# A four-layer network on one core: the first layer's experts run on the tokens that chose them, in 23 sorted tiles

## The chip, the cores and the metric

One core of one Trainium2 chip. The metric is the time of one execution in microseconds (us), the slowest core's, here the only one's. All data is 32-bit floating point unless a row says otherwise. Engines: PE (TensorE, matrix products), DVE (VectorE), ACT (ScalarE), POOL (GpSimd), SP (SyncE, which only issues transfers). PEld is PE's loading of the stationary operand.

## The reference, cut to what matters

Four layers, each `x = x + s * silu(g)` on 1024 tokens of 256 numbers, where `s` comes from a mixer and `g` from a feed-forward part, both of the normed `x`. The change touches only the first layer:

```python
# mixer: xh = xn @ W_in + b_in; gates by two block-diagonal products and sigmoid;
# complex decay a = exp(...), xc = sqrt(1 - a*a) * (xr + i*xi) * gate_x; h = linear scan of (a, xc) over 256 steps
# s = concat(h.real, h.imag) @ W_out + b_out
def _L0_ffn_ref(...):                       # 8 experts, each token takes 2
    shared = silu(x @ shared_gate_w) * (x @ shared_up_w) @ shared_down_w
    logits = x @ router_w
    top_val, top_idx = jax.lax.top_k(logits, K)                       # K = 2
    probs = jnp.zeros_like(logits).at[jnp.arange(T)[:, None], top_idx].set(jax.nn.sigmoid(top_val))
    xin = probs.T[:, :, None] * x[None]
    gu = jnp.einsum('etd,edf->etf', xin, gate_up_w)                   # 256 -> 2 * 128
    gate, up = jnp.split(gu, 2, axis=-1)
    h = jax.nn.silu(gate) * up
    expert_out = jnp.einsum('eti,eid->etd', h, down_w)                # 128 -> 256
    return shared + expert_out.sum(axis=0)
```

A token's weight is zero for the six experts that it did not choose, so their part of the sum is zero.

## The kernel before

Tokens are held as 8 tiles of 128 (`x_tok`, `xn_tok`), and turned, with features on the partitions, as `xnT`. PSUM is one tensor `banks` of 8 banks of 512 columns. The program is a row of stages (blocks); at the end of each all engines meet. The first block loads `x` and the first layer's weights: SP and ACT issue the transfers (ACT those of the list `late0`, L2796), and ACT then fetches its table of functions and warms it (L2798). `norm_stage` norms and turns `x`. Then `recurrent_layer_stage` does the whole first layer.

In that stage each engine has its own program, in the order in which it is written; semaphores join them. PE: `xh` (L444) with the router's logits (L450) between, the gates (L461), the turned choice weights (L468), the shared expert, and then 16 jobs, one for each of 8 experts and each half (512) of the tokens: `raise_` (L413, four products of 512 columns: gate and up) and `lower` (L421, four of 256 columns, summed in banks 0 to 3). DVE ranks the logits by comparing all pairs (`rank_mask`), then does the recurrence (about 35 operations of 128x1024, two scans and two reciprocals among them). Between its operations it does, for each job, `weigh` (L585, L587: gate and up times the token's weight) and `hidden` (L595). ACT does the sigmoids, sines and roots (`root`, L511) and each job's Silu (L507). The weights of the choices reach all partitions through DRAM (`probs_dram`). At the end PE multiplies `hT` by `W_out` (L489, `mix`), DVE and POOL add the bias (`add_bias`), DVE adds the gated result to `x_tok` (`add_gated`), and PE runs seven products on the identity that nothing reads (`keep_busy`, L494) before the stage's end.

The third layer's experts (L1370, L1843 and around) already gather tokens by an indirect transfer of POOL from `xn_dram`, with positions found by a running count (`top_mask`) and one-hot products.

## Time and profile before

| | us |
|---|---|
| median of 3 runs | 987.98 (985.75 to 992.25) |
| profiled execution, its time | 983.79 |
| its span, first to last instruction | 982.0 |
| PE busy | 922.5 (94%) |
| DVE busy | 685.5 (70%) |
| ACT busy | 478.2 (49%) |
| POOL busy | 289.7 (29%) |

The mean granted TensorE clock of the profiled execution is 0.995 of full speed. The first layer's stage runs from 15.6 to 142.2 us of the span. A row of the timeline gives start, duration, engine, line, operation, result<-operands with their shapes, a count of merged instructions, and in brackets how long the engine had sat idle before and what released it. `PEq`, `SPq` and so on are an engine's sequencer. One 32-bit product of 512 columns is two records of the trace.

### The profile page before, as it was taken

To read this page: it belongs to the slowest core of one execution; us is meant where nothing else is said; L and a number is where in the kernel's file an instruction comes from. 1 tells how busy PE (TensorE), PEld (TensorE's weight loads), DVE (VectorE), ACT (ScalarE), POOL (GpSimd) and SP (SyncE) were. 2 spreads that over 40 slices of the span, in tenths; PEclk is the share of its full clock that TensorE was granted. 3 is DMA by queue.
4 is the path that set the end of the run, shared out by engine and by line. 5 is a ranking of instruction groups with operands and counts; after the bars stand their busy time and mean duration, and the time that the engine had idled before them with its cause. 6 is when DMAs were issued, how large, how long until landed. Compare 5 with 4: busy or idle time off the path is not lost. (4 is left out here: it accounts for less than half of the span.)

```text
span 982.0 us, 13585 instructions
## 1 busy us (share of the span) xinstructions
PE 922.5 (94%) x4660; PEld 556.4 (57%) x4660; DVE 685.5 (70%) x1095; ACT 478.2 (49%) x1008; POOL 289.7 (29%) x254
## 2 busy tenths in 40 slices
PE   6999999999999999989999999989899899999997
PEld 3455564365566565655565555566466556555554
DVE  2889877368999999885635565576786735666552
ACT  3642224798888788444135555566665630111112
POOL 0000020007888788723013232103554420000000
PEclk9999999999999999999999999999999999999999
DMA  4123215041000000008454444201000002111101
GB/s 137 45 72 90 64 43 155 1 104 39 22 23 32 12 26 8 1 17 258 122 156 109 92 111 95 39 33 39 7 1 2 1 2 64 33 33 32 32 0 43
DMA packets 58303, 53.89 MB, mean 55 GB/s; under 512 B 14216, under 2 KB 53224, under 8 KB 58240
## 3 DMA queue, kind: packets, MB, share of 16 engines
q1 hardware_dynamic: 52704, 47.05, 16.2%
q0 software_dynamic: 3072, 4.20, 2.7%
q10 hardware_dynamic: 2464, 1.84, 0.6%
q8 instruction: 36, 0.59, 0.3%
q14 instruction: 27, 0.22, 0.1%
HBM read 44.45 MB, written 5.47 MB: 51 GB/s over the span
## 5 line engine op out<-in xcount | busy, mean ns | idle before, releaser
L1127 POOL TENSOR_TENSOR seen<-state,c_row 128x512 f32<-128x512 f32 x128 | 160.9, 1278 | 100.6 <-DVE state L1147 72.9
L1147 DVE TENSOR_TENSOR_SCAN state<-decay,banks 128x512 f32<-128x512 f32 x128 | 154.5, 1215 | 14.6 <-issue 7.1
L2646 PE MATMUL banks<-xnT,weight 128*128 128x512 f32 x256 | 115.2, 592 | 0.0
L1085 ACT ACTIVATE weighed_x<-dx_tok,b_tok 128x512 f32<-128x512 f32 x124 | 87.6, 709 | 26.4 <-PE banks L1263 25.1
L1095 ACT ACTIVATE decay<-delta_pairs,A 128x510 f32<-128x510 f32 x128 | 90.4, 707 | 6.2 <-DVE state L1147 6.2
L2299 POOL TENSOR_TENSOR prob<-prob,inverse 128x512 f32<-128x512 f32 x64 | 65.3, 1041 | 95.4 <-DVE inverse L2417 95.4
L1263 PEld LDWEIGHTS banks<-ident,weighed_x 128*128 128x128 f32 x512 | 58.3, 140 | 60.2 <-ACT weighed_x L1085 36.0
L2652 ACT ACTIVATE w_WqT<-banks 128x512 f32<-128x512 f32 x32 | 19.1, 597 | 149.2 <-PE banks L2646 149.2
L1263 PE MATMUL banks<-ident,weighed_x 128*128 128x128 f32 x512 | 80.1, 279 | 2.4 <-DVE state L1147 2.3
L2646 PEld LDWEIGHTS banks<-xnT,weight 128*128 128x128 f32 x256 | 48.6, 190 | 48.3 <-issue 46.7
L1277 PE MATMUL banks<-seen,fold 128*64 128x512 f32 x256 | 69.0, 618 | 0.0
L2658 DVE TENSOR_TENSOR inter<-w_WqT,banks 128x512 f32<-128x512 f32 x32 | 22.0, 688 | 66.7 <-ACT w_WqT L2652 66.1
L2480 ACT ACTIVATE prob<-banks,shift 128x256 f32<-128x256 f32 x128 | 59.2, 472 | 19.1 <-DVE probT L2424 9.0
L2017 DVE COPY probT<-banks 128x512 f32<-128x512 f32 x48 | 33.1, 690 | 45.2 <-PE banks L1891 40.6
L2704 PE MATMUL banks<-weight,inter 128*128 128x256 f32 x256 | 60.4, 379 | 1.1 <-PEq L2282 1.1
L2704 PEld LDWEIGHTS banks<-weight,inter 128*128 128x128 f32 x256 | 48.5, 190 | 20.9 <-issue 15.8
L413 PE MATMUL banks<-xnT,gate_up_w 128*128 128x512 f32 x128 | 57.6, 593 | 0.0
L2412 DVE TENSOR_REDUCE shift<-banks 128x2 f32<-128x512 f32 x64 | 40.9, 680 | 19.8 <-PE banks L2340 19.8
L2424 DVE STREAM_TRANSPOSE probT<-prob 128x512 f32<-128x512 f32 x64 | 44.1, 701 | 11.5 <-POOL prob L2299 11.5
L1843 POOL DMA_INDIRECT y_dram<-slot_result,slot_target x16 | 25.4, 1585 | 77.7 <-ACT slot_result L2092 77.7
L2073 ACT ACTIVATE prob<-banks,score_shift 128x128 f32<-128x128 f32 (+1 forms) x128 | 44.5, 423 | 1.4 <-DVE score_shift L2013 1.4
L2340 PE MATMUL banks<-latT,q_now 64*128 64x256 f32 x256 | 37.2, 409 | 7.7 <-ACT prob L2480 7.7
(395 smaller groups left out, 1687.9 us busy)
## 6 DMA issues: line engine op xcount, KB each, us to landing
prob_row<-probs_dram SPq DMA_DIRECT2D x8, 512.0 KB, 3.8
c_row<-c_dram SPq DMA_DIRECT2D x32, 128.0 KB, 2.9
slot_wide_w<-in_L_ffn_w_gate SPq DMA_DIRECT2D x16, 176.0 KB, 2.5
slot_wide_w<-in_L_ffn_w_up SPq DMA_DIRECT2D x16, 176.0 KB, 2.6
slot_down_w<-in_L_ffn_w_down SPq DMA_DIRECT2D x16, 176.0 KB
gate_up_w<-in_L_ffn_gate_up_w SPq DMA_DIRECT2D x8, 256.0 KB, 3.0
delta_pairs<-conv_in SPq DMA_DIRECT2D x8, 256.0 KB, 3.5
w_WqT<-in_L_attn_W_q SPq DMA_DIRECT2D x1, 2048.0 KB, 12.9
```

The source lines that it names most:

```text
L413: last = nc.tensor.matmul(banks[:, 4 + 2 * half + j, :], wide(j, k), xnT[:, k, cols[half]], start=(k == 0), stop=(k == KD - 1))
L1085: nc.scalar.activation(weighed[:, v % 2, tile, :, j, :], dx_tok[:, 4 * p + tile, :].rearrange("p (g e) -> p g e", g=groups), ACT.Identity, ...
L1095: nc.scalar.activation(decay[:, u % ring, :, 1:], delta[:, g, cols[p]].rearrange("p (b t) -> p b t", b=BATCH // 2)[:, :, 1:], ACT.Exp, sca ...
L1127: nc.gpsimd.tensor_tensor(seen[:, u % ring, :], state[:, u % ring, :], c_row[:, v % 4, :], ALU.mult).then_inc(seen_ready, 1)
L1147: nc.vector.tensor_tensor_scan(state[:, u % ring, :], decay[:, u % ring, :, :].rearrange("p b t -> p (b t)"), banks[:, 4 + u % 2, :], 0.0, ...
L1263: last = nc.tensor.transpose(banks[:, 4 + u % 2, tile * P:(tile + 1) * P], weighed[:, v % 2, tile, g, :, :].rearrange("p j e -> p (j e)"), ...
L1277: nc.tensor.matmul(banks[half, g // 2, :], fold[:, :], seen[:, u % ring, :], start=False, stop=(pair == STATES // 2 - 1), skip_group_check ...
L2073: last = nc.scalar.activation(dst[:, h, :], bank[:, h, :], ACT.Exp, bias=shift[:, u % 8, h:h + 1])
L2299: nc.gpsimd.tensor_tensor(two, two, inverse[:, u % 2, h, :].unsqueeze(2).broadcast_to([P, 2, SEQ]), ALU.mult).then_inc(prob_ready, 1)
L2480: last = nc.scalar.activation(prob[:, u % 2, h, qt * SEQ:(qt + 1) * SEQ], score_bank(u, h)[:, qt * SEQ:(qt + 1) * SEQ], ACT.Exp, bias=shif ...
L2646: last = self.nc.tensor.matmul(self.banks[:, pair + j, :], self.weights.weight[:, s, j, k, tile * P:(tile + 1) * P], self.xnT[:, k, self.c ...
L2704: last = nc.tensor.matmul(banks[:, t // 2, (t % 2) * D:(t % 2 + 1) * D], jobs.inter[:, tile, t * P:(t + 1) * P], weight[:, s, 2, tile, :], ...
```

## The change

The choices (2 of each of 1024 tokens, 2048 in all) are sorted by expert. Each expert's choices are padded up to tiles of 128 rows; (2048 + 8 * 127) / 128 gives at most 23 tiles. The number of tiles is fixed, whatever the data; a register holds each tile's expert, and the products take their weights at that register's address. All eight experts' weights now lie in SBUF. Tiles go in 12 groups of two (the last of one).

- SP stores the normed tokens to DRAM, loads all expert weights in 8 transfers, and stores each group's result rows to DRAM.
- DVE's routing is new: `top_mask`, a running place of every choice, then one-hot tensors; PE turns them by 16 products into a table (which token and which weight each slot of each tile has). PE reads 23 expert numbers into registers, then `keep_busy` with 4 products.
- POOL gathers 23 tiles of token rows. For a group: `turn_x` (PE), `keep_xT` (ACT), `raise_` (PE), `gate` (ACT, Silu with the slot's weight as scale), `middle` (DVE), `turn_mid` (PE), `keep_midT` (ACT), `lower` (PE), `keep_result` (ACT), store (SP). PE and ACT take the steps of several groups in turn; the 12 `middle` stand at fixed places in DVE's recurrence.
- When all results are stored, POOL gathers each token's two rows back: 16 transfers. PE adds them to the shared expert's part by products with the identity (`add_rows`). The bias is added by PE as well, into the banks of `mix`, so `add_bias` goes.
- ACT's list `late0` gets three more loads (`before`, `slots`, `choice_token`).

```diff
--- before.py
+++ after.py
...
-    jobs = 2 * (experts + 1)
+    choices = top * NT
+    tiles = (top * N + experts * (P - 1)) // P
+    groups = -(-tiles // 2)
+    size = [min(2, tiles - 2 * g) for g in range(groups)]
+    ring = 4
...
+                sp.dma_start(xn_dram.rearrange("(n p) d -> p n d", p=P), xn_tok[:, :, :]).then_inc(xn_stored, DMA)
+                for e in range(0, experts, 2):
+                    two = slice(e, e + 2)
+                    sp.dma_start(gate_up_w[:, two, :].rearrange("p e (k n) -> p (e k) n", k=KD),
+                                 gate_up[two, :, :].rearrange("e (k p) n -> p (e k) n", p=P)).then_inc(expert_weights_loaded, DMA)
+                    sp.dma_start(down_w[:, two, :], down[two, :, :].rearrange("e p n -> p e n")
+                                 ).then_inc(expert_weights_loaded, DMA)
+                for g in range(groups):
+                    sp.wait_ge(result_ready, g + 1)
+                    sp.dma_start(rows_dram[2 * g * P:(2 * g + size[g]) * P, :].rearrange("(a p) d -> p a d", p=P),
+                                 result[:, g % ring, 0:size[g], :]).then_inc(stored[g % ring], DMA)
...
+                def turn_x(g):
+                    pe.wait_ge(gathered[g % ring], DMA * tiles_to(g))
+                    if g >= 2:
+                        pe.wait_ge(xT_ready, g - 1)
+                    for k in range(KD):
+                        for j in range(size[g]):
+                            c = (2 * k + j) * P
+                            ins = nc.tensor.transpose(banks[:, g % 2, c:c + P], slot_x[:, g % ring, j, k * P:(k + 1) * P],
+                                                      ident[:, :])
+                    ins.then_inc(x_turned, 1)
...
+                def raise_(g):
+                    pe.wait_ge(xT_ready, g + 1)
+                    if g >= 2:
+                        pe.wait_ge(mid_ready, g - 1)
...
+                            ins = nc.tensor.matmul(
+                                banks[:, 2 + g % 2, j * 2 * width:(j + 1) * 2 * width], slot_xT[:, g % 2, k, j, :],
+                                gate_up_w[:, bass.ds(expert[2 * g + j], 1), k * 2 * width:(k + 1) * 2 * width].rearrange(
+                                    "p e n -> p (e n)"), start=(k == 0), stop=(k == KD - 1))
+                    ins.then_inc(raised, 1)
...
+                def add_rows(b):
+                    pe.wait_ge(rows_gathered[b], 2 * top * DMA)
+                    for t in (2 * b, 2 * b + 1):
+                        for r in range(top):
+                            ins = nc.tensor.matmul(banks[:, b, (t % 2) * D:(t % 2 + 1) * D], ident[:, :], rows[:, t, r, :],
+                                                   start=False, stop=(r == top - 1), skip_group_check=True)
+                    ins.then_inc(summed, 1)
...
+                pe.wait_ge(entries_ready, 2)
+                for n in range(choices):
+                    if n % (choices // 2) == 0:
+                        pe.wait_ge(one_hot_ready, n // (choices // 2) + 1)
+                    ins = nc.tensor.matmul(banks[:, 1, 0:2 * tiles], one_hot[:, n, :],
+                                           entry[:, n, :, :].rearrange("p i a -> p (i a)"), start=(n == 0), stop=(n == choices - 1))
+                ins.then_inc(table_done, 1)
+                pe.wait_ge(expert_index_ready, 1)
+                expert = [pe.value_load(expert_index[0:1, a:a + 1], min_val=0, max_val=experts - 1) for a in range(tiles)]
+                keep_busy(nc, banks[:, 3, :], ident, 4)
+                pe.wait_ge(expert_weights_loaded, DMA * experts)
+                turn_x(0)
+                pe.wait_ge(slot_prob_ready, 1)
+                for s in range(groups + 2):
+                    if s + 1 < groups:
+                        turn_x(s + 1)
+                    if s < groups:
+                        raise_(s)
+                    if s == 1:
+                        pe.wait_ge(shared_ready, 2)
+                    if 1 <= s <= groups:
+                        turn_mid(s - 1)
+                    if s >= 2:
+                        lower(s - 2)
+
+                pe.wait_ge(xT_ready, groups)
...
+                for b in range(2):
+                    add_rows(b)
                 pe.wait_ge(h_ready, 2)
-                for t in range(NT):
-                    for k in range(KD):
-                        last = nc.tensor.matmul(
-                            banks[:, 4 + t // 2, (t % 2) * D:(t % 2 + 1) * D], hT[:, k, t * P:(t + 1) * P],
-                            w["W_out"][:, k, :], start=(k == 0), stop=(k == KD - 1))
-                    last.then_inc(mixed, 1)
+                mix(0)
+                add_rows(2)
+                mix(1)
+                add_rows(3)
+                mix(2)
+                mix(3)
                 pe.wait_ge(gate_ready, 1)
                 keep_busy(nc, banks[:, 0, :], ident, 7)
...
+                for s in range(groups + 2):
+                    if s + 1 < groups:
+                        keep_xT(s + 1)
+                    if s < groups:
+                        gate(s)
+                    if 1 <= s <= groups:
+                        keep_midT(s - 1)
+                    if s >= 2:
+                        keep_result(s - 2)
+                    if s == 2:
+                        for q in range(4):
+                            act.wait_ge(angles_ready, q + 1)
+                            nc.scalar.activation(wave[:, q, :], wave[:, q, :], ACT.Sin, scale=two_pi).then_inc(waves_ready, 1)
+                    if s in (5, 6):
+                        root(s - 5)
...
+                pool.wait_ge(xn_stored, DMA)
+                pool.wait_ge(slot_token_ready, 1)
+                for a in range(tiles):
+                    g = a // 2
+                    if g >= ring:
+                        pool.wait_ge(x_turned, g - ring + 1)
+                    pool.indirect_dma_start(out=slot_x[:, g % ring, a % 2, :], out_offset=None, in_=xn_dram[:, :],
+                                            in_offset=bass.IndirectOffsetOnAxis(ap=slot_token[:, a:a + 1], axis=0)
+                                            ).then_inc(gathered[g % ring], DMA)
+                pool.wait_ge(row_index_ready, 1)
+                for r in range(ring):
+                    pool.wait_ge(stored[r], DMA * len(range(r, groups, ring)))
+                for t in range(NT):
+                    for r in range(top):
+                        pool.indirect_dma_start(out=rows[:, t, r, :], out_offset=None, in_=rows_dram[:, :],
+                                                in_offset=bass.IndirectOffsetOnAxis(ap=row_index[:, t, r:r + 1], axis=0)
+                                                ).then_inc(rows_gathered[t // 2], DMA)
 
             @block.vector
             def _(dve):
...
+                def middle(g):
+
+                    dve.wait_ge(silu_ready, g + 1)
+                    if g >= 2:
+                        dve.wait_ge(mid_turned, g - 1)
+                    for j in range(size[g]):
+                        ins = vector.scalar_tensor_tensor(
+                            mid[:, g % 2, j, :], banks[:, 2 + g % 2, j * 2 * width + width:(j + 1) * 2 * width],
+                            slot_prob[:, 2 * g + j:2 * g + j + 1], silu[:, g % 2, j, :], ALU.mult, ALU.mult)
+                    ins.then_inc(mid_ready, 1)
...
+                dve.wait_ge(table_done, 1)
+                vector.tensor_copy(slot_token[:, :], banks[:, 1, 0:tiles]).then_inc(slot_token_ready, 1)
+                vector.tensor_copy(slot_prob[:, :], banks[:, 1, tiles:2 * tiles]).then_inc(slot_prob_ready, 1)
+                dve.wait_ge(slot_prob_ready, 1)
...
+                shared(0)
+                shared(1)
+                angle(0)
+                angle(1)
+                middle(0)
...
+                steps.do(vector.tensor_tensor(ta[:, :], zr[:, :], zr[:, :], ALU.mult))
+                vector.tensor_tensor(ta[:, :], ta[:, :], tb[:, :], ALU.add).then_inc(square_ready, 1)
+                middle(4)
+                middle(5)
                 dve.wait_ge(modulus_ready, 1)
-                steps.do(nc.vector.tensor_tensor(tb[:, :], tc[:, :], zr[:, :], ALU.add))
-
-                nc.vector.tensor_scalar(ta[:, :], tb[:, :], 0.5, 1e-30, ALU.mult, ALU.max).then_inc(square_ready, 1)
-                hidden(2)
-                weigh(3)
+                steps.do(vector.tensor_tensor(tb[:, :], tc[:, :], zr[:, :], ALU.add))
+                vector.tensor_scalar(ta[:, :], tb[:, :], 0.5, 1e-30, ALU.mult, ALU.max).then_inc(square_ready, 1)
+                middle(6)
                 dve.wait_ge(modulus_ready, 2)
-                steps.do(nc.vector.reciprocal(tb[:, cols[0]], tc[:, cols[0]]))
-                hidden(3)
...
                 both(tb[:, :], zi[:, :], ALU.mult, sin)
-                hidden(7)
-                weigh(8)
+                middle(11)
                 both(tc[:, :], zi[:, :], ALU.mult, cos)
...
+    for name in ("before", "slots", "choice_token"):
+        add(name, list(A[name].shape), A[name], late)
```

The order of instructions at three places. First the start of ACT's queue, in the block before `norm_stage`: the last loads of `late0`, then the table and its warm-up (ACT's last work in the block). Before:

```order
L2796 DMA w_shared_up_w<-in_L_ffn_shared_up_w 128x2x128
L2796 DMA w_shared_down_w<-in_L_ffn_shared_down_w 128x256
L2798 ACT_TABLE_LOAD
L2798 ACTIVATE root_table<-root_table 128x1
L2777 UNCONDITIONAL_BRANCH
```

and of the change:

```order
L2954 DMA w_shared_down_w<-in_L_ffn_shared_down_w 128x256
L2954 DMA w_before<-in_before 128x128
L2954 DMA w_slots<-in_slots 128x128
L2954 DMA w_choice_token<-in_choice_token 128x16
L2956 ACT_TABLE_LOAD
L2956 ACTIVATE root_table<-root_table 128x1
```

Three issues now stand ahead of the table. Second, PE from the shared expert to its first routed products. Before (`L413` is `raise_`, `L421` is `lower`):

```order
L468 MATMUL banks<-ident,probs 8x128 x8
L413 MATMUL banks<-xnT,w_shared_gate_w 128x512 x2
L413 MATMUL banks<-xnT,w_shared_up_w 128x512 x2
L413 MATMUL banks<-xnT,gate_up_w 128x512 x4
L421 MATMUL banks<-w_shared_down_w,expert_hT 128x256 x4
```

and of the change (`L540` is the table, `L544` the read of a register, 23 times this load and pair in a row; `L437` is `turn_x`, `L447` `raise_`):

```order
L474 MATMUL banks<-xnT,w_shared_up_w 128x512 x2
L540 MATMUL banks<-entry,wave 128x46 x16
L544 TENSOR_LOAD tile_expert_index
L544 ISA x2
...
L242 MATMUL banks<-ident 128x512 x4
L437 MATMUL banks<-ident,slot_x 128x128 x8
L447 ISA
L447 MATMUL banks<-gate_up_w,slot_xT 128x256
```

Routed products followed the shared ones directly; now the table, the registers, `keep_busy` and two groups' gathered rows stand between. Third, DVE from the recurrence's first operation on. Before:

```order
L618 TENSOR_SCALAR turns<-gate_a,coef 128x1024
L620 SCALAR_TENSOR_TENSOR phi<-inside,turns 128x1024
L621 TENSOR_SCALAR ta<-turns 128x1024
L629 TENSOR_SCALAR tb<-ta 128x1024
L630 TENSOR_TENSOR angle<-ta,tb 128x1024
```

and of the change (`L798` waits for PE's table, `L720` is `middle`):

```order
L796 TENSOR_SCALAR turns<-gate_a,coef 128x1024
L798 CAST slot_token<-banks 128x23
L799 COPY slot_prob<-banks 128x23
L711 TENSOR_TENSOR shared_hT<-shared_silu,banks 128x512 x2
L804 TENSOR_SCALAR ta<-turns 128x1024
...
L720 SCALAR_TENSOR_TENSOR expert_mid<-banks,slot_prob,expert_silu 128x128 x2
L820 SCALAR_TENSOR_TENSOR phi<-inside,turns 128x1024
```

The wait for the table and the first `middle` now stand ahead of the scan `phi`.

## Rows read from the trace of the kernel before

**Rows 1.** Busy time by stretch (count of instructions), clock, DMA share, GB/s
```profile
70.00:120.00 50.00, 50.00 (x156) 28.69 (x155) 49.45 (x56) 13.35 (x16) 0.00 (x0) 1.00 0.25 76
```

**Rows 2.** Timeline, PE's job late in the stage, and the router's products
```profile
61.68 3.60 PE L413 MATMUL banks<-xnT,gate_up_w 128*128 128x512 f32 x8
65.11 1.89 PE L421 MATMUL banks<-down_w,expert_hT 128*128 128x256 f32 x8
66.84 3.60 PE L413 MATMUL banks<-xnT,gate_up_w 128*128 128x512 f32 x8
...
20.09 0.95 PE L450 MATMUL banks<-w_router_w,xnT 128*128 128x8 f32 x8
```

**Rows 3.** Timeline of DVE: a job's operations and the recurrence's
```profile
37.78 0.69 DVE L629 TENSOR_SCALAR tb<-ta 128x1024 f32<-128x1024 f32 x1
...
66.08 3.35 DVE L663 RECIPROCAL tb<-tc 128x512 f32<-128x512 f32 x1 [2.47 <-ACT tc L511]
...
85.31 0.68 DVE L595 TENSOR_TENSOR expert_hT<-expert_silu,expert_up 128x512 f32<-128x512 f32 x1
...
87.11 1.21 DVE L569 TENSOR_TENSOR zi<-radius,turns 128x1024 f32<-128x1024 f32 x1
...
103.00 2.28 DVE L701 TENSOR_TENSOR_SCAN zi<-radius,tc 128x1024 f32<-128x1024 f32 x1
```

**Rows 4.** Timeline of the stage's end and the next one's start
```profile
128.02 7.07 PE L489 MATMUL banks<-w_W_out,hT 128*128 128x256 f32 x32
...
137.51 3.60 PE L242 MATMUL banks<-ident 128*128 128x512 f32 x8
...
142.26 1.96 PE L242 MATMUL banks<-ident 128*128 128x512 f32 x4 [1.16 <-PEq L2814]
```

**Rows 5.** Timeline of the program's start, ACT's last loads and the first meeting
```profile
5.49 0.63 ACTq L2796 DMA_DIRECT2D w_shared_down_w<-in_L_ffn_shared_down_w  x1
...
6.15 1.28 ACT L2798 ACT_TABLE_LOAD   x1 [6.15 <-issue]
...
7.99 0.64 DVE L127 BATCH_NORM_AGGREGATE mean_var<-x_stats 128x2 f32<-128x6 f32 x8 [1.05 <-PEq L2777]
```

**Rows 6.** Timeline of the third layer's routing: a small operation of DVE
```profile
453.86 0.29 DVE L220 TENSOR_TENSOR above<-score,best 128x128 f32<-128x128 f32 x1
```

**Rows 7.** Timeline of the third layer's first gathers; last, all 16 as a group
```profile
499.45 1.17 POOL L1370 DMA_INDIRECT slot_x<-xn_dram,slot_token  x1 [38.60 <-DVE slot_token L1700]
...
500.93 0.97 POOL L1370 DMA_INDIRECT slot_x<-xn_dram,slot_token  x1 [0.30 <-issue]
...
502.46 0.44 PE L1944 MATMUL banks<-ident,slot_x 128*128 128x128 f32 x2 [1.06 <-DMA slot_x<-xn_dram,slot_token]
...
L1370 POOL DMA_INDIRECT slot_x<-xn_dram,slot_token x16 | 15.9, 997 | 53.6 <-DVE slot_token L1700 38.6 <-PE banks L1944 10.1 <-PE banks L1961 2.5
```

**Rows 8.** Transfers by line: count, KB each, median us from issue to landing
```profile
w_norm_w<-in_L_attn_norm_w SPq DMA_DIRECT2D x1, 1.0 KB, 1.7
...
out_dram<-x_tok SPq DMA_DIRECT2D x4, 256.0 KB, 2.1
```

**Rows 9.** Timeline of SP: an issue at a register's address
```profile
62.63 0.38 SPq L376 DMA_DIRECT2D gate_up_w<-in_L_ffn_gate_up_w  x1
```

**Rows 10.** ACT's groups: busy us, mean ns of one, idle before and its releaser
```profile
L2073 ACT ACTIVATE prob<-banks,score_shift 128x128 f32<-128x128 f32 x64 | 18.2, 374 | 1.4 <-DVE score_shift L2013 1.4
...
L2097 ACT ACTIVATE s_tok<-banks 128x512 f32<-128x512 f32 x3 | 1.8, 597 | 4.4 <-PE banks L1936 4.4
```

**Rows 11.** Timeline of ACT: a root of the recurrence
```profile
65.00 1.06 ACT L511 ACTIVATE tc<-ta 128x1024 f32<-128x1024 f32 x1
```

**Rows 12.** Timeline, DVE beside POOL and alone
```profile
133.72 1.27 POOL L272 TENSOR_TENSOR x_tok<-x_tok,s_tok 128x512 f32<-128x512 f32 x1
...
133.91 1.62 DVE L258 TENSOR_TENSOR x_tok<-x_tok,gated 128x512 f32<-128x512 f32 x1
...
136.95 0.69 DVE L258 TENSOR_TENSOR x_tok<-x_tok,gated 128x512 f32<-128x512 f32 x1
```

More of the change, by code:

```diff
@@ L481, in _ @@
[L481 to L492 removed]
+                                xh[:, k, cols[half]], start=(k == 0), stop=(k == KD - 1))
@@ L498, in shared @@
                 def shared(half):
[L500 to L507 removed]
+                    act.wait_ge(shared_raised, half + 1)
@@ L590, in hidden @@
[L590 to L598 removed]
+                    dve.wait_ge(shared_silu_ready, half + 1)
```

523 lines of the change are left out of this document (287 added, 236 removed).

## The prediction, made before the changed kernel was timed

> **What bounds the first layer now.** I read the busy time by stretch first. From 70 to 120 us PE is busy all 50.00 us and DVE 49.45 us, ACT 13.35, POOL none [rows 1]. The timeline says why. PE's job is `raise_` from 61.68 to 65.11 and `lower` to 66.84: 5.16 us each, so 0.86 us for a product of 512 columns and 0.43 for one of 256 [rows 2]. DVE's job costs 1.80 us (from `hidden` at 85.31 to the recurrence's next operation at 87.11) [rows 3], beside about 3.5 us of recurrence. Both engines are full together, so taking work from one alone gives little; the change takes from both. Then I read the stage's end: `mix` is done at 135.0 and `keep_busy` at 141.1; the next stage starts PE at 142.26, and only 1.16 us of idle time lie before it [rows 4]. PE's `keep_busy` ends the stage. So I ask when `mix` ends after the change.
>
> **What is removed.** 16 routed jobs: 82.6 us of PE and 29 us of DVE. A tile costs PE three products of 256 columns (two in `raise_`, one in `lower`) at 0.43, and three transposes of 128 columns; two of these span 0.44 [rows 7], so 0.22 at most, and I take 0.13 back to back. That is 1.7 us a tile, 39 for 23. `middle` costs DVE two short operations a group, 0.25 each (0.29 is the span of a 128x128 one [rows 6]): 6 us in all. If throughput were all, the stage would lose over 20 us. It is not, since what is added stands in a row. I walk through it, in the clock of before.
>
> **Start.** Three more issues come ahead of ACT's table load, which started at 6.15, as soon as the last issue (5.49, 0.63 long) was out; DVE, done early, waited 1.05 us for the meeting and went on at 7.99 [rows 5]. At about 0.53 us each everything shifts by 1.6 us. I add that at the end.
>
> **Routing.** PE starts at 15.7 (the row at 20.09 less two halves of `xh` and four router products [rows 2]). Two halves of `xh` and 16 logit products (0.24 each [rows 2]) end at 22.9. About 15 short operations of DVE, 0.2 each (a 128x128 one is 0.29 [rows 6], these are half as wide), give the mask at 25.8, and PE the places at 26.9. Another 30 short ones take 5.0 us, three operations 368 wide 1.3 and two one-hots of 128x1024 2.4 (1.21 each [rows 3]); with the expert numbers and `turns`, DVE is done at about 37. PE meanwhile: gates from 27.2 (`xh` is done at 26.4 and ACT has to copy it), 8 x 0.86, to 34.1, shared expert to 41.0, then the table's 16 products, priced like the router's plus some columns, 0.26 each: 45.2. DVE stands 8 us before `table_done`, and the whole recurrence stands behind it in DVE's queue.
>
> **Gathers.** The first starts at 45.5, the second 1.48 later (499.45 to 500.93), each further one 1.3 later (0.97 and 0.30 idle). The row comes to PE 3.0 us after the first's start (502.46) [rows 7]; I take that for all. Group 0 is there at 50.0, group 1 at 52.6, and `turn_x(1)` stands ahead of `raise_(0)`: 53.1 at the earliest.
>
> **Registers.** 23 times a register is read from SBUF, each with two checks. The trace has no such operation. Below: nothing. Above: a 1 KB transfer's 1.7 us [rows 8]. The nearest row is an issue of SP's sequencer at a register's address, 0.38 [rows 9]; I take 0.35. PE then reaches `raise_(0)` at 45.2 + 8.1 + 3.4 (`keep_busy`) + 1.0 = 57.7: 4.6 us later than the gathers would let it. Up to 0.15 us each they are hidden by the gathers; beyond, each 0.1 us costs 2.3 us.
>
> **The middle.** `raise_(0)` 1.7, two Silu of 128x128 0.8 (0.374 each [rows 10]), `middle(0)` 0.5: 60.9. DVE has waited since about 52. From here DVE sets the pace, not PE (3.4 us of products a group): `phi` 2.25, two angles 4.65, `xh` 2.3, the next three operations 2.4, four more 4.3, four `middle` 2.1 give 18.0, `middle(4)` done at 78.9 (from the 1.21, 0.69 and 2.28 of [rows 3]). Now, after `middle(5)`, DVE waits for ACT's first root, which stands behind `keep_midT(4)` and `keep_result(3)`: PE 1.2, ACT 0.65, a table load 1.28 [rows 5], the root 1.06 [rows 11], 4.4 in all: 83.3. Then `middle(6)` waits for ACT again: `keep_xT(7)` 0.6 [rows 10], the Silu table 1.28, two Silu 0.8, so it ends at 86.6. The second root, with two copies and a table load ahead, ends at 89.5. Two reciprocals at 3.35 [rows 3] and two `middle`: 97.2. Nine operations and three `middle`: 109.1. After `middle(11)` the recurrence needs 16.2 more (ten operations at 1.15 to 1.24, two scans): `h_ready` at 125.3.
>
> **The tail.** `turn_mid`, two ACT copies and `lower` take 2.5 from 109.1 and the store 2.1 [rows 8]: 113.8. Sixteen gathers follow on POOL alone; the last starts 1.48 + 14 x 1.3 = 19.7 later and lands at 136.5, 11 us after `h_ready`. `add_rows(3)` 1.7, `mix(2)` and `mix(3)` 3.45: 141.7. `keep_busy` 6.1: 147.8, against 141.1.
>
> **Sum.** 6.7 + 1.6 = 8.3 us more. The profiled execution's 983.8 (span 982.0 and 1.8 around it) becomes 992.1. The median of before is 4.2 above that execution, so I name 988.0 + 8.3 = 996.
>
> What I cost at nothing: 4 MB of transfers by SP from 17 us on (one of 256 KB takes 2.1 us to land [rows 8]; they have 30 us, and if they were late the first group would wait); the address arithmetic ahead of each dynamic product, about 70 times, hidden by the product before it (0.43) and by DVE's pace; `add_bias` gone, replaced by PE products before the rows land.
>
> **Two rules that speak against the change.** The only near row for the register reads is SP's 0.38 [rows 9]. The Trainium skill, "DMA: Bandwidth & Descriptors", section "Latency and other measured facts", gives a floor of about 600 ns for a `tensor_load`. As an estimate from that page the reads would take 13.8 us instead of 8.1, and the sum would be 1002. No run here shows it yet. The other concerns POOL beside DVE: the addition at 133.91 takes 1.62 us beside POOL's own addition at 133.72, and 0.69 alone [rows 12]. The Trainium skill, "SBUF — State Buffer", section "Who interferes with whom", says that the two share a port pair by an exclusive lock, and its trap is POOL's writing of descriptors under DVE's fast modes. By that rule, the trace agrees for arithmetic; for gathers no row tells.
>
> **Rivals.**
> - *Cheap registers.* At 0.15 us or less the reads hide under the gathers: 8.3 - 4.6 = 3.7 us more, 992. Chance 0.17.
> - *Dear registers, the other side.* At 0.7 us, twice what I take, they cost 16.1 - 3.4 = 12.7 instead of 4.6: 16.4 more than before, 1004; at 1.7 us, 39 more. It is slower by over 1% from 0.42 us a read. For: two checks stand behind each read, so the reads can't overlap. Against: SP's row. Chance 0.28.
> - *Gathers held up by DVE.* If each of POOL's gathers waits for the DVE operation in progress (about 1 us, as 1.62 - 0.69 in [rows 12]) while the recurrence runs, eight of the last sixteen lose 1 us each and the first group 2: 10 more than the forecast, 1006. Against: the third layer's gathers take 0.997 on average, with DVE at work beside most of them [rows 7]. Chance 0.10.
> - *DVE's waits vanish.* My walk has four waits of DVE, 8 at the table, 8 at `middle(0)`, 4 and 3 at the roots. If 20 of these 23 us were an error, `mix` would end 12 us earlier than before: 976. Each follows from the order in a queue, so I give it little. Chance 0.08.
> - *The forecast*, reads between 0.15 and 0.42: 992 to 998. Chance 0.37.
>
> **Numbers.** A measurement of this kernel can tell about 1%, 9.9 us. Faster by more: 0.08. Slower by more: dear registers 0.28, held gathers 0.10, and 0.02 of the forecast's edge: 0.40. Within 1%: 0.52. The range reaches from the cheap side less 5 us (gathers without the 0.30 gap save 16 x 0.3) to held gathers plus half of the dear case: 985 to 1012.
>
> **What would show it.** The next stage starts near 150.5. DVE idle about 8 us at the table and about 8 at `middle(0)`; 23 reads between the table and `keep_busy`, their sum read off PE's gap; `phi` starting near 62; roots waited for by DVE; sixteen gathers of 1.3 us after the last store, and PE released by them in `add_rows`. It is wrong if `h_ready` comes before 115, if the gathers' pitch is not 1.3, or if a later stage changes.

## The result, and the profile after

| | before | changed |
|---|---|---|
| median of four runs, us | 987.53 (985.75 to 992.25) | 1012.07 (1009.04 to 1015.08) |
| profiled execution, its span | 982.0 | 1013.2 |
| PE busy | 922.5 (94%) | 915.7 (90%) |
| DVE busy | 685.5 (70%) | 665.9 (66%) |
| POOL busy | 289.7 (29%) | 329.9 (33%) |
| mean granted clock of TensorE | 0.995 | 0.968 |

The changed kernel takes 1.023 times as long as before (95% interval 1.0189 to 1.027), 24.5 us more at the median. I had forecast 996 with a range to 1012. The side was one of my rivals', the size beyond either of them.

Where the two profiles part is read from the first row of DVE in each stage, which is released by an engine's sequencer (PEq) when all have met. All rows of a timeline below have the columns of those before: start, duration, engine, line, operation, result and operands, count, and in brackets the idle time before and its releaser. Timeline of DVE, changed kernel, one row for each of the first norm, the first layer's stage, the second layer's norm, the third layer's routing and the stage behind it:

```profile
11.48 0.64 DVE L127 BATCH_NORM_AGGREGATE mean_var<-x_stats 128x2 f32<-128x6 f32 x8 [4.50 <-PEq L2935]
...
19.44 0.35 DVE L734 COPY same_row<-earlier 128x64 f32<-128x64 f32 x1 [3.92 <-PEq L106]
...
163.56 0.64 DVE L127 BATCH_NORM_AGGREGATE mean_var<-x_stats 128x2 f32<-128x6 f32 x8 [4.70 <-PEq L2972]
...
469.30 0.24 DVE L1811 CAST before_bf<-w_before 128x128 bf16<-128x128 f32 x1 [5.97 <-PEq L106]
...
535.18 0.23 DVE L2200 CAST ident_bf<-ident 128x128 bf16<-128x128 f32 x1 [4.81 <-PEq L1625]
```

The norm starts 3.5 us later than in [rows 5], the second layer 21.3 later than in [rows 4]. But the third layer's routing, from the fourth row to the fifth, takes 65.88 us, and it is not touched by the change. Before it took 56.94:

```profile
445.45 0.24 DVE L1653 CAST before_bf<-w_before 128x128 bf16<-128x128 f32 x1 [5.11 <-PEq L106]
...
502.39 0.23 DVE L2042 CAST ident_bf<-ident 128x128 bf16<-128x128 f32 x1 [2.85 <-PEq L1467]
```

In the changed kernel's profile the granted clock falls to half there. Busy time by stretch, changed kernel, PE alone (length, PE busy and its count, granted clock, share of DMA, GB/s):

```profile
509.00:514.00 5.00, 3.96 (x41) 0.80 0.00 0
514.00:529.00 15.00, 15.00 (x121) 0.50 0.01 1
```

That is the first question for the experiments. The others are in the first layer. ACT's queue at the start, then PE from the table to the first expert product:

```profile
6.71 1.93 ACTq L2954 DMA_DIRECT2D w_before<-in_before  x1
8.67 0.46 ACTq L2954 DMA_DIRECT2D w_slots<-in_slots  x1
9.15 0.45 ACTq L2954 DMA_DIRECT2D w_choice_token<-in_choice_token  x1
9.64 1.28 ACT L2956 ACT_TABLE_LOAD   x1 [9.64 <-issue]
```

```profile
44.74 3.67 PE L540 MATMUL banks<-entry,wave 128*128 128x46 f32 x32
61.30 5.47 PE L242 MATMUL banks<-ident 128*128 128x512 f32 x8 [12.90 <-issue]
...
67.99 1.99 PE L447 MATMUL banks<-gate_up_w,slot_xT 128*128 x8 [0.34 <-ACT slot_xT L593]
```

The three issues are 2.84 us in place of my 1.6: the first of them holds the queue for 1.93. They also begin 0.56 us later than the table load did before (6.71 against 6.15), since the issue of `w_shared_up_w` ahead of them took 0.98 instead of 0.51. PE stands 12.90 us where the 23 reads are, 0.56 us each, and the four products of `keep_busy` behind them take 5.47 us instead of the 3.4 I used. The windows say why:

```profile
48.00:54.00 6.00, 0.41 (x4) 0.77 0.14 44
54.00:60.00 6.00, 0.00 (x0) 0.50 0.40 108
60.00:66.00 6.00, 4.70 (x7) 0.59 0.08 23
```

The granted clock is at 0.50 while PE stands, which is 1.2 GHz of 2.4, and still low when it works again. DVE's waits came where I had put them, the second twice as long:

```profile
48.51 0.18 DVE L798 CAST slot_token<-banks 128x23 uint32<-128x23 f32 x1 [7.90 <-PE banks L540]
...
70.76 0.61 DVE L720 SCALAR_TENSOR_TENSOR expert_mid<-banks,slot_prob,expert_silu 128x128 f32<-128x128 f32 x2 [15.35 <-ACT expert_silu L602]
...
94.03 1.23 DVE L843 TENSOR_TENSOR tb<-tc,zr 128x1024 f32<-128x1024 f32 x1 [3.90 <-ACT tc L622]
```

In the tail, POOL's row gathers (L695) beside DVE's last operations, POOL's rows first:

```profile
127.42 1.88 POOL L695 DMA_INDIRECT gate_up_w<-expert_rows,row_index  x1 [0.30 <-issue]
...
130.93 1.96 POOL L695 DMA_INDIRECT gate_up_w<-expert_rows,row_index  x1 [0.30 <-issue]
133.20 0.95 POOL L695 DMA_INDIRECT gate_up_w<-expert_rows,row_index  x1 [0.30 <-issue]
134.45 1.98 POOL L695 DMA_INDIRECT gate_up_w<-expert_rows,row_index  x1 [0.30 <-issue]
...
147.98 0.95 POOL L695 DMA_INDIRECT gate_up_w<-expert_rows,row_index  x1 [0.30 <-issue]
...
126.28 2.27 DVE L874 TENSOR_TENSOR_SCAN zi<-radius,tc 128x1024 f32<-128x1024 f32 x1
...
130.86 1.22 DVE L706 TENSOR_TENSOR tc<-zr,wave 128x1024 f32<-128x1024 f32 x1
...
134.39 1.22 DVE L882 TENSOR_TENSOR hT<-tc,td 128x1024 f32<-128x1024 f32 x1
```

While DVE works, gathers take 0.95 to 1.98 us; once it is done at 135.61, all take 0.95. And PE at the stage's end:

```profile
119.65 2.90 PE L466 MATMUL banks<-down_w,expert_midT 128*128 x6
...
134.69 3.78 PE L490 MATMUL banks<-gate_up_w,ident 128*128 128x256 f32 x8 [5.00 <-DMA gate_up_w<-expert_rows,row_index]
...
156.07 6.17 PE L242 MATMUL banks<-ident 128*128 128x512 f32 x14
163.55 1.96 PE L242 MATMUL banks<-ident 128*128 128x512 f32 x4 [1.30 <-PEq L2972]
```

### The profile page after: what moved, and what is told of

Its sections match the earlier page's. It is cut to its first block and busy times, and to the rows that moved or that the text cites. A ratio compares the mean times of both kernels' runs of the same rounds, so it can differ in the third digit from the quotient of the medians.

```text
span 1013.2 us, 13799 instructions
## 1 busy us (share of the span) xinstructions
PE 915.7 (90%) x4687; PEld 564.4 (56%) x4687; DVE 665.9 (66%) x1109; ACT 483.0 (48%) x1043; POOL 329.9 (33%) x292
## 3 DMA queue, kind: packets, MB, share of 16 engines
q10 hardware_dynamic: 2896, 1.98, 0.6%
## 5 line engine op out<-in xcount | busy, mean ns | idle before, releaser
L2175 DVE COPY probT<-banks 128x512 f32<-128x512 f32 x48 | 33.1, 691 | 45.2 <-PE banks L2049 44.8
L242 PE MATMUL banks<-ident 128*128 128x512 f32 x56 | 31.5, 703 | 30.0 <-issue 12.9
L2582 DVE STREAM_TRANSPOSE probT<-prob 128x512 f32<-128x512 f32 x64 | 44.2, 701 | 11.7 <-POOL prob L2457 11.7
```

Of the source, the lines that this page charges most:

```text
L2582: nc.vector.transpose(probT[:, b % 2, h, unit, :], prob[:, u % 2, h, :]).then_inc(flipped, 1)
```

## The experiments

Unless said otherwise each is the changed kernel with one edit. Ratios are against before, with 95% intervals.

### Is the fall in the third layer the change's?

The changed kernel again:

> The changed kernel once more, unaltered, so that the runs beside it have it on the same chip. Theory 1 (the drop of the granted clock to 0.50 at 514 to 529 us belongs to this program): the profiled execution shows it again, route from norm2 to attention takes 64 to 67 us, and the ratio to the kernel before is 1.02 to 1.027. Theory 2 (it fell into one execution by chance): the third layer's routing takes 57 to 58 us as before, and the ratio is 1.015 to 1.02.

Measured: 1014.58 us, ratio 1.0229 (1.0175 to 1.0282). The profiled execution (1014.98) has the routing at 65.87 us again. So theory 1 seemed right, and would have been the wrong conclusion: the four times were 1014.98, 1014.75, 1014.41 and 1008.29, the last at a mean clock of 0.977 instead of 0.968. Before, too, had times near 985.4 (clock 0.994) and near 991.7 (0.986). So more executions of before were profiled.

> The kernel before, unaltered, for a second profile of it. Its times so far lie in two groups, near 985.4 (granted clock 0.994) and near 991.7 (0.985). Theory (the fall of the granted clock in the third layer's routing comes to this kernel too, and is no work of the change): where the profiled execution is of the second group, the routing from the cast of the ordering matrix to that of the identity takes 63 to 66 us instead of 56.9, with the clock at 0.50 in it. Rival: the 6 us lie elsewhere (the scan, the last layers).

Measured: the profiled one took 985.32, its routing 58.6 us. Two more, with the same theory and rival, took 985.68 and 985.14. Three more:

> The kernel before once more for its profile. If the execution takes 991 to 993: theory, its third layer's routing takes 63 to 66 us with a granted clock of 0.50 in it; rival, the routing takes 57 to 59 and the 6 us lie elsewhere.

That one took 986.84 (routing 56.94) and the next 985.85. The last:

> The same kernel for a profile again; theory and rival are those of the looks before: at 991 to 993 the third layer's routing takes 63 to 66 us, or it takes 57 to 59.

Measured: 992.01 us. Its windows, PE alone, and DVE's rows at both ends of the routing:

```profile
487.00:492.00 5.00, 4.89 (x51) 0.70 0.01 3
492.00:497.00 5.00, 5.00 (x43) 0.50 0.00 0
497.00:502.00 5.00, 5.00 (x43) 0.50 0.00 0
```

```profile
446.37 0.24 DVE L1653 CAST before_bf<-w_before 128x128 bf16<-128x128 f32 x1 [5.21 <-PEq L106]
...
512.23 0.23 DVE L2042 CAST ident_bf<-ident 128x128 bf16<-128x128 f32 x1 [4.69 <-PEq L1467]
```

65.86 us, as in the changed kernel. The fall behind the short idle time is not the change's; it comes to some executions of either kernel and costs 6 us in the total. It follows that the profile of before in the first part had drawn the good case and that of the changed kernel the bad one. Set against this execution (span 990.2), the changed one (1013.2) is 23.0 us longer. Of these, 22.2 are there when the second layer starts (141.38 against 163.56), 22.2 when the scan ends (437.12 and 459.30) and 22.95 when the routing does. The change costs 23 us, nearly all in the start and the first layer. Why one execution falls and another doesn't, these runs don't show. No execution of the changed kernel itself without the fall was profiled; that there are such rests on the times near 1009 with the higher mean clock.

Two smaller things differ between executions whatever the kernel, and the differences below have to be read with them. The second layer takes 294.0 us in two of the seven profiles of before and 295.7 in the five others. And the norm's stage takes 6.9 to 7.7 us in before and 6.7 to 8.2 in the changed kernel and its versions, so the first layer's stage can start over a microsecond earlier or later without an edit ahead of it.

### The reads

```diff
-                expert = [pe.value_load(expert_index[0:1, a:a + 1], min_val=0, max_val=experts - 1) for a in range(tiles)]
+                expert = [min(a // 3, experts - 1) for a in range(tiles)]
```

> The expert of each tile is a constant in the program instead of a register read from SBUF; tiles so meet a wrong expert now and then, all shapes and counts stay. Theory (the 12.9 us in which PE stands between the table and keep_busy are the 23 reads): the gap goes, the gathers bind raise_(0) instead (group 1 lands near 57), middle(0) starts near 60 instead of 70.8 and the second layer starts 10 to 11.5 us earlier; the time falls by 10 to 13 us. Rival (the gap is something else, the 4 MB of expert weights arriving for instance): keep_busy or turn_x(0) still wait until 61 or later, and the time falls by less than 3 us.

Measured: ratio 1.0128 (1.0089 to 1.0167); the profiled execution takes 1001.72 against 1015.08, both with the fall in the third layer. PE, and DVE at the second layer's start:

```profile
46.62 3.68 PE L242 MATMUL banks<-ident 128*128 128x512 f32 x8
...
56.25 2.96 PE L447 MATMUL banks<-gate_up_w,slot_xT 128*128 128x256 f32 x8
...
152.72 0.64 DVE L127 BATCH_NORM_AGGREGATE mean_var<-x_stats 128x2 f32<-128x6 f32 x8 [4.71 <-PEq L2972]
```

The gap is gone, `keep_busy` takes its 3.68, and `raise_(0)` starts 11.7 us earlier, now held by the gathers. The second layer starts 10.8 us earlier. Of these, 1.6 are not the edit's: the first layer's stage starts at 17.84 instead of 19.44. That leaves 9.2, somewhat less than the 10 to 11.5 expected, and the second layer itself takes 1.7 less here (294.0 instead of 295.7). The theory holds in its cause: the gap is the reads.

What a read consists of:

```diff
-                expert = [pe.value_load(expert_index[0:1, a:a + 1], min_val=0, max_val=experts - 1) for a in range(tiles)]
+                expert = [pe.value_load(expert_index[0:1, a:a + 1]) for a in range(tiles)]
```

> The 23 reads without the two checks of the value's bounds behind each. Theory (the checks make a part of the 0.56 us, since each needs the value that has just arrived): the gap before keep_busy falls from 12.9 to 5 to 9 us and the second layer starts 4 to 8 us earlier. Rival (it is the load from SBUF itself, and reads do not overlap): the gap stays at 12 to 13 us and nothing moves by more than 1 us.

```profile
53.53 6.59 PE L242 MATMUL banks<-ident 128*128 128x512 f32 x8 [6.38 <-issue]
```

The gap is 6.38: 0.28 us for a load, and 0.28 for its two checks. The second layer starts at 157.25, 6.3 us earlier, 1.25 of them because the first layer's stage starts earlier; ratio 1.0155 (1.0117 to 1.0193). The theory holds. `keep_busy` takes 6.59 here, nearly all of it at half clock: the clock was no better for the shorter wait.

Reads beside products. First, one product on the identity behind each read:

```diff
+                    expert.append(pe.value_load(expert_index[0:1, a:a + 1], min_val=0, max_val=experts - 1))
+                    keep_busy(nc, banks[:, 3, :], ident, 1)
```

> The changed kernel with one 512-column product on the identity behind each of the 23 reads, so PE works while its sequencer reads. Theory (the clock fell to 0.50 because PE stood still, and a product of 0.43 hides under a read of 0.56): the row of reads still takes 12.9 to 14 us, keep_busy takes 3.4 us instead of 5.5, the granted clock stays 1.00 up to raise_(0), and the second layer starts 1.5 to 3 us earlier. Rival 1 (read and product add up): the row takes 22 us and the time grows by 8 to 9 us. Rival 2 (the clock falls there whatever PE does): keep_busy keeps its 5.5 us.

```profile
47.74 23.42 PE L242 MATMUL banks<-ident 128*128 128x512 f32 x54
...
54.00:60.00 6.00, 6.00 (x15) 1.00 0.37 105
```

My expectation had the product wrong: 0.43 is one of its two records, a product is 0.86. With 0.86 the row reads plainly: 27 products (54 records) in 23.42 us are 0.87 each, so the 23 reads cost nothing beside them. PE's sequencer reads while the array works, and the clock stays at 1.00: those two parts of the theory hold. Its numbers don't: the row is 20.0 us long, near rival 1's 22, but because 23 products are 19.8 us and not because read and product add up. The second layer starts at 167.94, 4.4 later; ratio 1.0249 (1.0204 to 1.0295).

So the reads can go beside work that is there anyway. DVE computes the experts right behind the tiles' ends, and each 512-column product of the gates and the shared expert, from the third on, is followed by one or two reads:

```diff
+                def product_done():
+                    behind[0] += 1
+                    if behind[0] == 3:
+                        pe.wait_ge(expert_index_ready, 1)
+                    if behind[0] >= 3:
+                        read(1 + behind[0] % 2)
```

> The expert numbers are worked out by DVE right behind the tiles' ends, and PE's 23 reads stand one or two at a time behind the products of the gates and of the shared expert, from the third on, all still read. Theory (PE's sequencer reads while the array works, so a read of 0.56 us hides under a product of 0.43 to 0.86): the gap before keep_busy goes, the products grow by 1 to 4 us together, the second layer starts 8 to 11 us earlier, the time falls by 8 to 12 us. Rival (a read holds the array too, because the queue has to run dry first): the table is done 10 to 13 us later than 48.4, and the time stays within 2 us of the changed kernel's.

```profile
51.06 3.68 PE L242 MATMUL banks<-ident 128*128 128x512 f32 x8
...
60.64 3.62 PE L447 MATMUL banks<-gate_up_w,slot_xT 128*128 x8
```

The gap is gone. The table is done 2.8 us later, since two reads (1.12) are longer than a product (0.86). `raise_(0)` starts 7.3 us earlier, the second layer 5.7 (below my 8), the time is 8.2 us lower where both show their lower mean clock (1006.5 against 1014.7), ratio 1.0171 (1.0128 to 1.0213). The profiled execution was not one of these: it took 1000.97, without the fall in the third layer. That the gap can be hidden is shown; the gain in the layer is below the theory's range.

### The start

The three loads in SP's queue, behind its own, then at the head of the layer's stage:

```diff
                     sp.dma_start(dst, src).then_inc(loaded, DMA)
+                for dst, src in extra0:
+                    sp.dma_start(dst, src).then_inc(late_loaded, DMA)
```

> The three loads that the change adds to ACT's queue are issued by SP behind its own. Theory (they hold ACT's table load, for which everybody waits at the end of the first block): the first norm goes back from 11.48 to about 8 us, everything behind it 3.5 us earlier, the time falls by 3 to 3.5 us. Rival (the start is later because more transfers share the DMA engines, whoever issues them): the norm still starts at 10.5 or later, and the time changes by less than 1 us.

Measured: the norm at 9.45, 2.0 us earlier, the layer's stage 3.3 earlier, the second layer only 2.3 earlier, ratio 1.0175 (1.0119 to 1.0231). Between theory and rival. ACT's table load is back at 6.15, but now SP comes late: there too the first of the three, issued at 5.94, holds its queue 1.56 us.

```diff
             def _(sp):
+                for dst, src in tables:
+                    sp.dma_start(dst, src).then_inc(tables_loaded, DMA)
                 sp.dma_start(xn_dram.rearrange("(n p) d -> p n d", p=P), xn_tok[:, :, :]).then_inc(xn_stored, DMA)
```

> The changed kernel with its three added loads issued by SP at the head of the first layer's stage, behind a semaphore of their own, instead of on ACT's queue in the first block. Theory (the whole later start is these three issues and what they delay): the norm starts at 8.0 us as before and the layer's stage at 15.0 to 15.7, the second layer starts 3.5 to 4.5 us earlier than with the changed kernel, and nothing waits for the tables at 28 us. Rival (a part of the later start comes from elsewhere, the larger program for instance): the norm starts at 9.5 or later as with the loads on SP's queue ahead of the meeting.

```profile
8.03 0.64 DVE L127 BATCH_NORM_AGGREGATE mean_var<-x_stats 128x2 f32<-128x6 f32 x8 [0.96 <-PEq L2940]
...
15.66 0.22 DVE L738 COPY same_row<-earlier 128x64 f32<-128x64 f32 x1 [3.59 <-PEq L106]
```

Both starts are those of before; the second layer starts 4.0 us earlier. The theory holds: the three loads are the whole later start. The total doesn't resolve it (ratio 1.0228, 1.0174 to 1.0281): three of its four times have the fall in the third layer, 1010.8 to 1012.5, against 1014.4 to 1015.1.

### The row gathers

```diff
                 middle(11)
-                both(tc[:, :], zi[:, :], ALU.mult, cos)
...
-                both(td[:, :], zi[:, :], ALU.mult, cos)
                 steps.join()
```

> Leaves out DVE's twelve operations of the recurrence behind the last middle (only the two that write hT stay), so POOL's row gathers run beside an idle DVE. Theory (a gather that meets a DVE operation with two SBUF inputs is held up to 1 us): all sixteen take 0.95 us, the last starts 18.8 us after the first instead of 22.35, and the second layer starts 3.0 to 3.6 us earlier. Rival (the long gathers are long for their descriptors or for the stores before them): single ones still take 1.4 to 2.0, the last starts 22 or more behind the first, and the second layer moves by less than 1 us.

```profile
125.60 0.94 POOL L695 DMA_INDIRECT gate_up_w<-expert_rows,row_index  x1 [32.98 <-DMA expert_rows<-expert_result]
...
143.10 1.41 POOL L695 DMA_INDIRECT gate_up_w<-expert_rows,row_index  x1 [0.30 <-issue]
```

Fifteen of sixteen take 0.94 or 0.95; the one of 1.41 stands beside `add_gated`. The last starts 19.2 us after the first instead of 22.35, the second layer at 160.39, 3.2 earlier; ratio 1.0204 (1.0165 to 1.0243). The theory holds.

### All together

Late loads on SP, reads among the products, the table between the shared expert's halves, the angles ahead of DVE's wait for the table, `phi` and the gate products ahead of `middle(0)`, the middles closer together, the roots taken by ACT at the third and fourth group, `mix(b)` ahead of `add_rows(b)`:

```diff
+                angle(0)
+                angle(1)
                 dve.wait_ge(table_done, 1)
...
-                    if s in (5, 6):
-                        root(s - 5)
+                    if s in (2, 3):
+                        root(s - 2)
...
+                for b in range(NT // 2):
+                    mix(b)
+                    add_rows(b)
```

> All causes mended at once: late loads on SP, expert numbers early and the reads among PE's products, the table ahead of the second half of the shared expert, DVE's angles ahead of the table and phi and the gate products ahead of the first middle, the middles 3.5 to 4 us apart so that the last comes about 10 us ahead of h_ready, the two roots taken by ACT at the third and fourth group, mix between the additions of rows. Theory (every piece was on the path): last middle near 103, row gathers from 108 on, last of them near 128, the second layer starts at 138 to 143 against 142.3 before, and the time is 978 to 988 where before takes 985.4. Rival (the gathers held by DVE, or ACT's queue with its table loads, set a pace of over 4.3 us a group): last middle at 110 or later, second layer at 147 or later, time 992 or more.

Measured: ratio 0.9998 (0.9964 to 1.0033), 985.16 to 996.98. Last `middle` at 106.1, the last row gather at 130.90, the second layer at 145.49. By the ratio all the 23 us are back, but the kernel is not faster. The profiled execution was one of the slowest (996.71); in it the second layer starts 18.1 us earlier than in the changed kernel and still 3.2 later than before. Between theory and rival.

Then the tables at the stage's head, `phi` ahead of the wait and one angle behind it, two products in PE's last wait, and 4 products at the end instead of 7:

> The combined version with four further edits: the three tables are loaded by SP at the head of the first layer's stage behind a semaphore of their own (in no queue ahead of the first meeting), phi stands ahead of the wait for the table and angle(1) behind it, two products fill PE's wait ahead of the last addition of rows, and keep_busy at the stage's end has 4 products instead of 7. Theory (start 1.7 us, first gathers 2 us, end 3.8 us, all on the path): norm at 8.0 to 8.5 us, raise_(0) near 54, second layer at 137 to 140, time 977 to 981 where before takes 985.4. Rival (the short keep_busy lets the granted clock fall at the second layer's start and gives back what it saves): prepare takes 67.9 us instead of 66.2 or more, time 983 or more.

```profile
132.62 3.60 PE L242 MATMUL banks<-ident 128*128 128x512 f32 x8
137.53 1.96 PE L242 MATMUL banks<-ident 128*128 128x512 f32 x4 [1.31 <-PEq L2998]
```

The second layer starts at 137.54, 4.7 us earlier than before. The time is 980.45 at best where before's best is 983.52, ratio 0.9963 (0.9932 to 0.9994): a third of a percent faster, with an interval that ends just below 1. At its best the time lies at the upper end of the theory's range, at the median (986.82) in the rival's. The rival named the preparation of the scan, the first stage of the second layer behind its norm: it takes 67.9 us in this profile, and 66.2 in the first profile of before. But that is no mark of the short `keep_busy`, since the changed kernel (seven products) and five of the seven profiles of before show the same 67.9.

## Why the prediction was wrong, point by point

The step that failed was the sum's term for the registers: 0.35 us a read, taken from an issue of SP's sequencer, where a read with its checks took 0.56. Three smaller terms failed beside it: the clock behind the standing PE, which the sum didn't have, DVE holding the row gathers, which it priced at nothing, and the start.

My walk against the profile, the latter less 3.8, its later stage start (19.44 against 15.65); a `middle` is done where DVE's next operation starts:

| | predicted | measured | later by |
|---|---|---|---|
| table done | 45.2 | 44.6 | -0.6 |
| `raise_(0)` | 57.7 | 64.2 | 6.5 |
| `middle(0)` done | 60.9 | 67.5 | 6.6 |
| first root in DVE's hands | 83.3 | 90.2 | 6.9 |
| `middle(8)` done | 97.2 | 103.6 | 6.4 |
| `h_ready` | 125.3 | 131.8 | 6.5 |
| first row gather | 113.8 | 121.8 | 8.0 |
| last row gather starts | 133.5 | 144.2 | 10.7 |
| `mix` done | 141.7 | 152.4 | 10.7 |

**Right:** the order of events. DVE idle 8 at the table (7.90), both waits at the roots (4 and 3: 3.90 and 2.52), DVE and not PE setting the pace from there, the row gathers ending after `h_ready`, transfers of 4 MB hidden. From `middle(0)` to `h_ready`, 64 us, the walk is off by 0.1.

**Registers, the term that failed first.** 0.35 a read by an issue of SP's sequencer [rows 9]; it is 0.56, half of it the checks: 12.9 instead of 8.1, so 4.8 more. An issue is not a load with two checks behind it, and no row of before was any nearer. The rival *dear registers* (0.42 us a read and more) was true; I had given it a chance of 0.28. The Trainium skill, "DMA: Bandwidth & Descriptors", section "Latency and other measured facts", gives about 600 ns as the floor of such a load. The read with its checks, 0.56, is near it, and the sum by it (1002) was nearer than mine; but the load alone, 0.28, is well below that floor.

**Clock, absent from the sum.** I priced `keep_busy` at 3.4 by rows of a PE that had never stood still. PE stood 12.9 us, the granted clock was 0.50, and the products took 5.47: 2.0 more. The same at the tail, where `lower(11)` stands in the path. PE alone:

```profile
119.65:122.55 2.90, 2.90 (x8) 0.50 0.00 0
```

Six records of `lower` take 2.90 us there and 1.56 at full clock in the first combined version. From the last `middle` to the first row gather it is 6.3 us here and 5.5 in that version: 0.9 of the 1.5 that I was off. The clock is at 0.51 on average from 133 to 147 as well, where `add_rows` takes 3.78 us instead of 1.89, but there PE waits for the gathers anyway.

**Gathers held by DVE.** A rival with a chance of 0.10, and true, but smaller than I priced it: the span from the first to the last of the sixteen is 22.35 instead of 19.7, 2.7 more, and with the recurrence taken away it is 19.2, so the holding costs 3.2. My argument against it misread [rows 7]: single gathers of that group take 0.94 to 1.17, so none was held for long, but DVE's operations beside them in the trace are mostly short or read PSUM; none is a 1.2 us operation between SBUF tensors as in the recurrence. The rows couldn't speak on this case. The rival stood as an alternative to the dear registers; both came. The range was also added up wrongly: 1006 and half of the dear registers' 8 more are 1010, and 992 less 5 is 987, not 1012 and 985.

**Start.** 1.6 forecast, 3.5 measured at the norm and 3.8 at the layer's stage. Three times a usual issue was right for two of them; the first took 1.93, and 0.56 came from an issue ahead of them.

**Later stages.** I named a later stage's change as a sign against me. The profiles showed one (9 us in the routing), and it was none of the change's: the same fall is in a profile of before. What is left there of the 23 us is 0.8.

**Sum.** 6.5 to `raise_(0)`, 1.5 to the first row gather, 2.7 among the gathers are 10.7; 2.2 in the start; 8.3 that I had. That gives 21.2 for the second layer's start, and 21.3 was measured against the profile I had used (22.2 against the other, whose first layer's stage starts 0.9 earlier). Of the 12.9 that I had not forecast, 4.8 are the reads and 2.0 the clock behind them. Added to 996 they give 1009, where two of the four executions lie (1009.04, 1009.3); the other two, near 1015, have the lower mean clock that goes with the third layer's fall, and the median stands between.

## What to carry to other kernels

A sequencer's reads and checks cost the engine nothing behind a product that is longer than they are, and everything when they stand alone; look where they stand before pricing them. Add to a stall on PE what the lower clock does to the work behind it, and let rivals add up in the range where nothing makes them exclude each other. Before a difference in an untouched stage is explained, look at a second profile of each kernel, best one with the same total: here a single pair of profiles showed 31 us where the change made 23. And before a gain is laid to an edit, take off what was already there when the edited stage started.

## What the runs showed of the hardware

- PE's sequencer needs 0.28 us to load a register from SBUF and 0.28 for two bound checks (12.90 and 6.38 us for 23). Behind products of 0.86 the 23 reads vanish (27 products in 23.42 us).
- A gather that starts while DVE is inside one of the recurrence's operations seems to wait for that operation's end and then take some 0.8 us: the one at 134.45 ended at 136.43, 0.82 after the DVE operation of 134.39; the one at 130.93 ended 0.81 after that of 130.86; the one at 127.42 ended 0.75 after the scan of 126.28. Not every overlap holds it (133.20 took 0.95, DVE's operation started behind it). Two operands in SBUF are not the condition: in the changed kernel an operation with one tensor operand, 0.69 us for 1024 columns, held one too, whose end came 0.81 behind it.

```profile
53.46 0.69 DVE L810 TENSOR_SCALAR tb<-ta 128x1024 f32<-128x1024 f32 x1
...
53.85 1.11 POOL L687 DMA_INDIRECT slot_x<-xn_dram,slot_token  x1 [0.30 <-issue]
```

  What the condition is stays open: in before's third layer, a one-operand operation on int32 (at 580.12, 0.94 long) did not hold the gather at 580.26 (0.99). Reciprocals didn't hold any. In the first combined version, POOL's rows and the DVE operations beside them:

```profile
70.39 1.97 POOL L706 DMA_INDIRECT slot_x<-xn_dram,slot_token  x1 [0.31 <-issue]
...
76.41 0.95 POOL L706 DMA_INDIRECT slot_x<-xn_dram,slot_token  x1 [0.30 <-issue]
...
70.28 1.23 DVE L858 TENSOR_TENSOR tb<-tc,zr 128x1024 f32<-128x1024 f32 x1 [0.60 <-ACT tc L636]
...
75.83 3.35 DVE L862 RECIPROCAL tb<-tc 128x512 f32<-128x512 f32 x1 [2.52 <-ACT tc L636]
```

  By the rule in the Trainium skill, "SBUF — State Buffer", section "Who interferes with whom", that DVE and GpSimd share a port pair by an exclusive lock, this is what would come; the trace agrees, and puts the price for a gather at up to 1.03 us beside an operation of 1.2 us. Beside the scan `phi` (2.28 long) a gather took 2.99 in the run with the reads among the products, 2.04 more.
- One issue of a load at about 6.5 us took 1.93 us on ACT's queue and 1.56 on SP's, where most of its neighbours took 0.43 to 0.5. It goes neither with the queue nor with the load: in the first combined version, on SP's queue, `w_before` at 5.92 took 0.78 and `w_slots` at 6.75 took 1.87. At the head of the layer's stage, at 15.61, `w_before` took 0.33. The long issue ended at 7.5 to 8.6 in each case; what it waits for was not tried.
- With PE idle for 12.90 us the granted clock was 0.50 and still 0.59 on average in the next 6 us. In the third layer's routing it fell to 0.50 for at least 15 us of full work in one of the seven profiles of before and in both of the changed kernel, and over that stretch it stayed at 1.00 in the other six of before. I found no difference ahead of it that tells which.
